# Wider tiles of the tensor engine in an audio tower: 64x128 projections, 64-column tiles for turned mixtures, output product and logits, 32x64 mixing

## The chip, the cores and the metric

One core of one Trainium2 chip runs the whole kernel in one launch. The metric is the device time of that launch in microseconds (us). All data are float32 but for two small causal masks in bfloat16.

## What is computed

The input is x of shape 128 x 64 x 750 (batch, feature, time). The result h has shape 128 x 94 x 64.

```python
# pooling to tokens: windows of 8 time steps, softmax of the window's scores
scores = einsum('bwkf,of->bwko', xp, w) + b
h = sum(xp * softmax(scores, axis=2), axis=2)                # (128, 94, 64)

# attention, 8 heads of rank 32, no causal mask
n = layernorm(h)
q, k = einsum('btd,hrd->bhtr', n, Q), einsum('bud,hrd->bhur', n, K)
attn = softmax(einsum('bhtr,bhur->bhtu', q, k) / sqrt(64), -1)
h = h + einsum('bhtd,hde->bte', einsum('bhtu,bud->bhtd', attn, n), VO)

# second layer: 4 heads of width 16, 4 experts each with its own query, causal
sx = einsum('bsh,ndh->bnsd', layernorm(h), hl_w) + hl_b
att = softmax(einsum('bnesd,bntd->bnest', q(sx, wq), k(sx, wk)) * 4 + causal, -1)
out = where(sx == 0, 0, einsum('bnest,bntd->bnesd', att, v(sx, wv)))
gs = softmax(einsum('bnsf,nef->bnse', out, gate_w) + gate_b, -1)
hn = layernorm(einsum('bnsed,bnse->bnsd', out, gs) + sx[n, n])   # the residual is batch n of head n
hx = masked two-layer net on hn; fout = layernorm(hx + hn)
h = h + fout * softmax(fout @ fgate_w.T, -1) per head
```

## The kernel before, in words

The batch is worked off in quads: four batch items at a time, 32 quads. The 94 tokens of an item are padded to 96 and cut into three blocks of 32, so that a tile of 128 partitions holds one block of four items. The work on one quad is spread over thirteen steps of a software pipeline that is written out by hand: each engine has a function `quad(g)`, called for g = 0 to 43, and in it stands, in a fixed order, what the engine does in that step, each piece for another quad (`g - 3`, `g - 7` and so on). Engines run their lists in order and meet only through semaphores; a wait stands before the piece that needs it. Nothing is moved at run time.

In step g TensorE (PE) does, in this order, with the line of the products in brackets:

- turns of exponentials for the second layer (turn_p3, L766), logits of the head (head_logits, L797), turns of x (turn, L588), a turn of fx (turn_rest, L803);
- mix3 (L776), the second layer's mixture over tokens, on 32x32 tiles;
- turn_x (L650), two more turn_p3, **turn_c(0)** (L785), score3_b (L752 the mask, L759 the scores), **turn_c(1)**, **turn_c(2)**, pool_x (L606, 128x32 tiles), front_turn (L703), two more turn_p3, layer1 (L807);
- **project** twice (L657), **front_pair(0)** (L710), front_sv (L716, L719), score(0) (L665), **front_pair(2)**, score(1), the last three functions on 64x32 tiles;
- **mix** (L676), layer2 (L811), score(2) (L665), **give_outT** (L686), with even g tok_score (L598, 128x32 tiles), with odd g a turn of token weights (L612), give_out (L697), score3_a (L737, L743), turns of x and of fo (L588, L790).

A tile is named rows x columns: rows are the partitions of the contraction, columns those of the weights and of the output. What the pieces in bold do:

- project: keys of the attention. The weights `g_w` have 128 columns of 64 rows, in two halves of the partitions. Before, a call takes four column tiles of 32 for each half: 8 products of 384 moving columns. ACT copies each call's result (copy_k, L1068); score(0) waits for both copies.
- front_pair: keys of the second layer for two experts, from weights `aq` of 4 heads x 32 columns: 8 products of 384 columns per call. ACT copies them (front_kp, L1101). mix waits for the copy of front_pair(2), whose banks it writes, and so does exp_s(0), which stands behind it in ACT's list.
- mix: attention weights times tokens, for 3 blocks, 2 parities of the heads, 2 halves of the 64 features and 4 items: 48 products of 384 columns on 32x32 tiles, weights `xn`. ACT copies the result (copy_cT, L1079) after exp_s(0) (L1074); exp_s(1), copy_oT, with odd g the copy of token weights, exp_s(2) follow.
- give_outT: the product with VO, accumulated over 4 pairs of heads: 16 products of 192 columns on 128x32 tiles.
- turn_c: turns the second layer's mixture back to tokens and applies a constant matrix `gx` with the gate's weights. For each of 4 experts and 4 blocks of 32 tokens the weights are a slice of `ct3`, in which the expert is the innermost dimension, and 84 columns of `gx` move: 16 products per call on 128x32 tiles.
- head_logits: 8 products of 12 columns on 96x32 tiles.

Two lines of layout matter for the steps:

```python
ct3 = sb("ct3", [128, NJ, 128, NE])        # NE = 4
xn = sb("xn", [128, 4, NJ, 2, NFEAT])      # NFEAT = 64
```

A float32 product appears in the trace as two MATMUL records and two LDWEIGHTS records (weight loads; engine PEld).

VectorE (DVE) holds the reductions, the shifts before exponentials (soft: L1368 the maximum, L1370 the subtraction), the guards (L1375) and transposes of 32x32 blocks (L1349). mix3 waits for soft(2), which needs score3_a. DVE also waits for layer2 in mask_second (L1440), after which score(2) may write its bank. ScalarE (ACT) holds exponentials and copies out of PSUM. GpSimd (POOL) holds elementwise work on SBUF; `residual` writes ft (z_made) and `norm_affine(.., 0, ..)` writes fx. SyncE (SP) issues two x loads of 375 KB per quad (L332) and eight stores (L380, L382). Instructions themselves come by DMA as well, through queues of the kind "instruction".

Of the kernel before, what the change touches and what calls it, by code (L numbers as in the profile page):

```python
# [15 lines left out]
TP = 96  # L16
HEADS, RANK = 8, 32
NH, NE, HD = 4, 4, 16
QB = 32
# [10 lines left out]
def exists(m, total):  # L30

    return not isinstance(m, int) or 0 <= m < total
# [10 lines left out]
def audio_tower(nc, x, tok_w, tok_b, attn_q, attn_k, attn_vo, hl_w, hl_b, wq, wk, wv, gate_w, gate_b,  # L43
                ln_g, ln_b, fc1_w, fc1_b, fc2_w, fc2_b, fnorm_g, fnorm_b, fgate_w, out):
    with ExitStack() as ctx:
# [7 lines left out]
        psum = ctx.enter_context(nc.psum_tensor("psum", [128, 8, 512], F32))  # L53
# [9 lines left out]
        g_w = sb("g_w", [128, 2, 128])  # L63
        vo_w = sb("vo_w", [128, HEADS // 2, NFEAT])
# [51 lines left out]
        HP = HEADS // 2  # L116
        TAIL = 29
        NT = 3
        TB = 32
        NJ = 3  # L120
# [6 lines left out]
        xn = sb("xn", [128, 4, NJ, 2, NFEAT])  # L127
        xT = sb("xT", [128, 2, 4, TP])
# [5 lines left out]
        pT = sb("pT", [128, NT, 2, HP, NT, TB])  # L134
        cT = sb("cT", [128, HP, NT, 4, TB])
        oT = sb("oT", [128, NT, 2, TB])
        cen = sb("cen", [HD, HD])
        aq = sb("aq", [128, NE, NH, 32])
# [8 lines left out]
        fgw = sb("fgw", [96, 2, NJ * NH])  # L147
        foT = sb("foT", [96, 256])
# [17 lines left out]
        x3T = sb("x3T", [128, 4, TP])  # L166
# [123 lines left out]
        z_made = sem("z_made")  # L290
# [17 lines left out]
        fo_made_late = sem("fo_made_late")  # L308
# [94 lines left out]
        def _(pool):  # L403
# [28 lines left out]
            for n in range(NH):  # L432
                rows = slice(QB * n, QB * n + QB)
# [67 lines left out]
            def norm_affine(g, k, done, order, dst):  # L501

                y = yc[:, k, :].rearrange("p (a d) -> p a d", d=HD)
                pool.tensor_tensor(y, y, bcast(gam[:, k, :], 1, NJ * NH), ALU.mult).then_inc(done, 1)
                pool.wait_ge(done, 2 * g + 1)
                y = yc[:, k, :].rearrange("p (" + order + " c) -> p " + order + " c", c=32, h=2)
                pool.tensor_tensor(dst, y,
                                   bcast(bcast(bet[:, k, :], 1, y.shape[2]), 1, y.shape[1]), ALU.add).then_inc(done, 1)
# [15 lines left out]
            def quad(g):  # L524
                if exists(g - 11, TAIL):
                    finish(g - 11)
                if exists(g, NQUAD):
                    if g < 4:
                        pool.wait_ge(tok_ready, (g) // 2 + 1)
                    weigh(g)  # L530
                if exists(g - 9, TAIL):
                    pool.wait_ge(z_mul, g - 8)
                    norm_affine(g - 9, 1, fo_made, "h j", fo[:, (g - 9) % FR, :].rearrange("p (j h c) -> p h j c", j=NJ, h=2))
                if exists(g - 2, NQUAD):
                    pool.wait_ge(at_summed, 3 * g - 3)
                    norm_p(1, at_normed)
                if exists(g - 2, NQUAD):
                    norm_p(2, at_normed)
                if exists(g - 6, NQUAD):
                    pool.wait_ge(y_eps, g - 5)  # L540
                    norm_power(g - 6, 0, y_rstd)
                if exists(g, NQUAD):
                    pool.wait_ge(ln_stat, 2 * g + 2)
                    ln_power(g)
                if exists(g - 6, TAIL):
                    pool.wait_ge(y_rstd, 2 * g - 10)
                    scale(0, y_mul)
                if exists(g - 5, NQUAD):
                    pool.wait_ge(l_inv, g - 4)
                    gate_scale((g - 5) % 2)  # L550
                if exists(g - 1, NQUAD):
                    pool.wait_ge(at_summed, 3 * g - 2)
                    norm_p(0, at_normed)
                if exists(g - 7, TAIL):
                    pool.wait_ge(t_made, g - 6)
                    residual()
                if exists(g - 8, NQUAD):
                    if g - 8 >= 28:
                        pool.wait_ge(z_eps, g - 7)
                    norm_power(g - 8, 1, z_rstd)  # L560
                if exists(g - 5, NQUAD):
                    pool.wait_ge(g_inv, 2 * g - 8)
                    gate_weight(g - 5)
                if exists(g - 6, TAIL):
                    norm_affine(g - 6, 0, fx_made, "j h", fx[:, :, 0:96].rearrange("p h (j c) -> p j h c", c=32))
                if exists(g - 5, NQUAD):
                    pool.wait_ge(g_weight, 2 * g - 8)
                    gate_mul((g - 5) % 2)
                if exists(g, NQUAD):
                    pool.wait_ge(ln_rstd, 2 * g + 2)  # L570
                    ln_apply(g, (g) % 4)
                if exists(g - 2, NQUAD):
                    pool.wait_ge(ln3_var, 2 * g - 2)
                    power3(g - 2)
                if exists(g - 8, TAIL):
                    scale(1, z_mul)
# [5 lines left out]
        def _(pe):  # L582
# [68 lines left out]
                mm.then_inc(at_turned, 1)  # L651

            def project(n, i, bank, done):
                for c in range(4):
                    for half in range(2):
                        rows = slice(64 * half, 64 * half + 64)
                        mm = pe.matmul(psum[32 * c:32 * c + 32, bank + half, 0:4 * TP], g_w[rows, i, 32 * c:32 * c + 32],  # L657
                                       xT[rows, n % 2, :, :].rearrange("p b t -> p (b t)"), start=True, stop=True)
                mm.then_inc(done, 1)

            def score(n, j, bank, done):
# [6 lines left out]

            def mix(n, bank):
                for ub in range(NT):  # L670
                    for par in range(2):
                        for c in range(2):
                            for b in range(4):
                                rows = slice(TB * b, TB * b + TB)
                                q = 64 * par + 32 * c
                                mm = pe.matmul(psum[q:q + 32, bank + b, 0:HP * TP].rearrange("p (h j t) -> p h j t", h=HP, j=NT),  # L676
                                               xn[rows, n % 4, ub, 0, 32 * c:32 * c + 32],
                                               pT[rows, :, par, :, ub, :].rearrange("p j h t -> p h j t"), start=(ub == 0), stop=(ub == NT - 1))
                mm.then_inc(at_mixed, 1)

            def give_outT(bank):
                for hp in range(HP):
                    for half in range(2):
                        for c in range(2):
                            q = 64 * half + 32 * c
                            mm = pe.matmul(psum[q:q + 32, bank, 0:NT * 64].rearrange("p (j c) -> p j c", j=NT), vo_w[:, hp, 32 * c:32 * c + 32],  # L686
                                           cT[:, hp, :, 2 * half:2 * half + 2, :].rearrange("p j b t -> p j (b t)"),
                                           start=(hp == 0), stop=(hp == HP - 1))
                mm.then_inc(at_outT, 1)

            def give_out(bank):
# [12 lines left out]
                mm.then_inc(f_turned, 1)  # L704

            def front_pair(e, bank, done):
                for n in range(NH):
                    for half in range(2):
                        rows = slice(64 * half, 64 * half + 64)
                        mm = pe.matmul(psum[32 * n:32 * n + 32, bank + half, 0:NJ * 128], aq[rows, e + half, n, :],  # L710
                                       x3T[rows, :, :].rearrange("p b t -> p (b t)"), start=True, stop=True)
                mm.then_inc(done, 1)

            def front_sv(bank):
# [65 lines left out]

            def turn_c(j, bank, done):
                for e in range(NE):
                    for b in range(4):
                        rows = slice(QB * b, QB * b + QB)
                        mm = pe.matmul(psum[rows, bank, GC * e:GC * e + GC], ct3[:, j, rows, e], gx[:, e, :], start=True, stop=True)  # L785
                mm.then_inc(done, 1)

# [4 lines left out]

            def head_logits(bank):
                for h in range(2):
                    for c in range(4):
                        rows = slice(QB * c, QB * c + QB)
                        mm = pe.matmul(psum[rows, bank, 0:NJ * NH], foT[:, 128 * h + QB * c:128 * h + QB * c + QB], fgw[:, h, :],  # L797
                                       start=(h == 0), stop=(h == 1))
                mm.then_inc(fl_made, 1)

# [468 lines left out]
        def _(dve):  # L1269
# [54 lines left out]
            for n in range(NH):  # L1324
                rows = slice(32 * n, 32 * n + HD)
# [129 lines left out]
            def quad(g):  # L1455
# [40 lines left out]
                if exists(g - 6, NQUAD):  # L1496
                    soft(g - 6, 1, 0, s_shifted1)
                if exists(g - 10, NQUAD):
                    if 1 <= g - 10 < 30:
                        dve.wait_ge(fo_made, 2 * g - 20)  # L1500
                    centre(g - 10)
# [95 lines left out]
```

## Time and profile before

| | |
|---|---|
| median of 3 runs | 1020.71 us (1018.73 to 1024.64) |
| profiled execution | 1028.39 us |
| its span, first to last instruction | 1026.7 us |
| mean granted clock of TensorE | 0.963 |
| busy: PE / DVE / ACT / POOL | 85% / 73% / 72% / 68% |
| PE records | 23616 matmul, 23616 weight load |

The chain is the work that ended last, followed back from the end; its shares say through which engine the end was reached. Busy time of PE is modelled: matmuls overlap, and the time of a record includes a latency during which the next one already streams. Idle time is listed before the instruction that ended it, with what released it; "issue" means that the engine waited for nothing that the profile shows.

### The profile page before, as it was taken

The page shows a single profiled execution, that of the slowest core. Times are in us where ns is not written, and L with a number is a line of the kernel's source. Part 1 is how long each engine was busy: PE and PEld are TensorE (multiplying, and loading weights), DVE is VectorE, ACT ScalarE, POOL GpSimd, SP SyncE. Part 2 cuts the span into 40 slices and gives each one's busy share as a digit, 9 for nine tenths or more (in the row PEclk, how much of TensorE's full clock was granted, in tenths as well). Part 3 has the DMA queues.
Part 4 walks back from the last instruction along what each step waited for, and adds up shares of the span by engine and source line. Part 5 has one row for each costly group of instructions (what it writes and reads, how often), then busy time and mean ns, then how long its engine had stood idle before and what let it go on. Part 6 is the DMA issues. An engine that isn't in the chain of part 4 may idle for free.

```text
span 1026.7 us, 53493 instructions
## 1 busy us (share of the span) xinstructions
PE 875.7 (85%) x23616; PEld 602.5 (59%) x23616; DVE 754.3 (73%) x1786; ACT 741.7 (72%) x2631; POOL 693.8 (68%) x1087
## 2 busy tenths in 40 slices
PE   4488988998898989899999999998998998887853
PEld 3365655665665656566676666665676665555531
DVE  2346677777777788778888788877888888776765
ACT  1567777887777888777887788887887787774521
POOL 3343345666678677677788777776777877766684
PEclk9789999999999999999999999999999999999965
DMA  6211111001111110011111111001000000000000
GB/s 191 66 62 33 33 34 33 27 11 33 33 33 37 38 36 24 18 38 37 38 38 38 37 37 38 15 27 41 7 9 7 7 7 7 4 8 6 11 8 21
DMA packets 34504, 31.47 MB, mean 31 GB/s; under 512 B 26080, under 2 KB 26080, under 8 KB 34272
## 3 DMA queue, kind: packets, MB, share of 16 engines
q1 hardware_dynamic: 33926, 28.00, 9.4%
q8 instruction: 185, 3.03, 1.2%
q14 instruction: 47, 0.39, 0.1%
q10 hardware_dynamic: 250, 0.05, 0.0%
q0 software_dynamic: 96, 0.00, 0.0%
HBM read 24.95 MB, written 3.08 MB: 27 GB/s over the span
## 4 chain that ended last, share of the span: by engine, by line
PE 62%; ACT 17%; DVE 11%; issue 4%; SPq 4%; POOL 2%; DMA 0%; POOLq 0%
PE psum L676 8%; ACT pu L1074 8%; PE psum L776 7%; PE psum L785 6%; PE psum L766 6%; PE psum L657 4%; PE psum L759 4%; PE psum L710 4%; DVE pu L1370 4%; DVE mx L1368 4%; ACT cT L1079 3%; PE psum L665 3%; SPq L346 2%; PE psum L606 2%; ACT kp L1101 2%
## 5 line engine op out<-in xcount | busy, mean ns | idle before, releaser
L1074 ACT ACTIVATE pu<-psum,mx 128x94 f32<-128x94 f32 x768 | 250.7, 386 | 4.0 <-DVE mx L1343 4.0
L1074 ACT ACTIVATION_READ_ACCUMULATOR pu<-psum,mx 128x1 f32 x768 | 194.7, 254 | 0.0
L462 POOL TENSOR_TENSOR pu<-pu,pr 128x752 f32<-128x752 f32 x96 | 137.4, 1445 | 23.9 <-DVE pr L1346 23.8
L1368 DVE TENSOR_REDUCE mx<-psum 128x16 f32<-128x1536 f32 (+2 forms) x96 | 117.2, 1221 | 48.3 <-PE psum L759 30.7
L495 POOL TENSOR_TENSOR st<-st,neg_half 128x12 f32<-128x12 f32 x64 | 146.2, 2285 | 5.0
L448 POOL TENSOR_TENSOR ln_ve<-ln_mv,eps_c 128x3 f32<-128x3 f32 x32 | 6.2, 193 | 178.8 <-DVE ln_mv L1338 178.8
L1343 DVE TENSOR_REDUCE mx<-psum 128x8 f32<-128x752 f32 x96 | 89.0, 927 | 46.1 <-PE psum L665 46.1
L1370 DVE TENSOR_TENSOR pu<-psum,mx 128x1536 f32<-128x1536 f32 (+2 forms) x96 | 117.6, 1225 | 3.3
L665 PE MATMUL psum<-kp,xT 64*32 64x376 f32 x1536 | 103.1, 486 | 17.4 <-DVE ft L1440 11.6
L1112 ACT ACTIVATE pT<-psum 128x512 f32<-128x512 f32 x192 | 104.5, 595 | 14.4 <-PE psum L766 12.5
L766 PE MATMUL psum<-ident_w,pu 128*128 128x128 f32 x768 | 102.1, 277 | 1.0 <-ACT pu L1074 0.6
L676 PE MATMUL psum<-pT,xn 32*32 32x384 f32 x3072 | 88.5, 491 | 9.6 <-ACT kp L1101 8.6
L1349 DVE STREAM_TRANSPOSE pT<-pu 128x768 f32<-128x768 f32 x96 | 89.7, 958 | 4.5 <-POOL pu L462 4.5
L766 PEld LDWEIGHTS psum<-ident_w,pu 128*128 128x128 f32 x768 | 87.6, 142 | 3.9 <-ACT pu L1074 1.2
L1375 DVE SCALAR_TENSOR_TENSOR ct<-sxT,psum 128x512 f32<-128x512 f32 x96 | 60.3, 684 | 32.3 <-PE psum L776 32.3
L785 PE MATMUL psum<-gx,ct 128*32 128x84 f32 x3072 | 74.1, 242 | 8.2 <-issue 6.7
L776 PE MATMUL psum<-pT,vv 32*32 32x384 f32 (+2 forms) x3072 | 70.9, 403 | 10.9 <-DVE pu L1370 9.7
L676 PEld LDWEIGHTS psum<-pT,xn 32*32 32x32 f32 x3072 | 45.2, 103 | 52.4 <-ACT kp L1101 30.7
L785 PEld LDWEIGHTS psum<-gx,ct 128*32 128x32 f32 x3072 | 61.9, 139 | 21.8 <-issue 19.5
L1115 ACT ACTIVATE oc<-psum 128x336 f32<-128x336 f32 x96 | 43.3, 452 | 38.8 <-PE psum L785 32.1
L1064 ACT ACTIVATE xT<-psum 128x384 f32<-128x384 f32 x32 | 15.7, 491 | 72.5 <-PE psum L650 72.4
L710 PE MATMUL psum<-x3T,aq 64*32 64x384 f32 x1024 | 65.8, 483 | 1.2 <-ACT hx L1121 1.2
(185 smaller groups left out, 2123.8 us busy)
## 6 DMA issues: line engine op xcount, KB each, us to landing
xs<-in_x SPq DMA_DIRECT2D x64, 375.0 KB, 3.8
out_h<-ho SPq DMA_DIRECT2D x126, 16.0 KB, 1.8
out_h<-ho SPq DMA_DIRECT2D x126, 7.5 KB, 1.8
gx<-in_L_ffn_gate_w SPq DMA_DIRECT2D x16, 0.2 KB
fc<-in_L_ffn_fc_w SPq DMA_DIRECT2D x12, 1.0 KB
fc<-in_L_ffn_fc_b SPq DMA_DIRECT2D x12, 0.1 KB
vo_w<-in_L_attn_VO SPq DMA_DIRECT2D x2, 64.0 KB, 8.7
q_w<-in_L_attn_Q SPq DMA_DIRECT2D x1, 64.0 KB, 7.8
```

The costliest lines, as they stand in the source:

```text
L462: pool.tensor_tensor(p, p, bcast(pr[:, j, :, :].rearrange("p a b -> p (a b)"), 2, NTOK), ALU.mult).then_inc(done, 1)
L495: pool.tensor_tensor(st[:, k, 3, :], st[:, k, 2, :], neg_half[:, 0:NJ * NH], ALU.pow).then_inc(rstd, 1)
L665: mm = pe.matmul(psum[TB * b:TB * b + TB, bank + par, 0:HP * NTOK], xT[rows, n % 2, b, TB * j:TB * j + TB], kp[rows, n % 2, b, :, 0:NTOK], ...
L676: mm = pe.matmul(psum[q:q + 32, bank + b, 0:HP * TP].rearrange("p (h j t) -> p h j t", h=HP, j=NT), xn[rows, n % 4, ub, 0, 32 * c:32 * c + ...
L710: mm = pe.matmul(psum[32 * n:32 * n + 32, bank + half, 0:NJ * 128], aq[rows, e + half, n, :], x3T[rows, :, :].rearrange("p b t -> p (b t)" ...
L766: mm = pe.transpose(psum[:, bank, 128 * e:128 * e + 128], pu3[j][:, e, k, :, :].rearrange("p b u -> p (b u)"), ident)
L776: mm = pe.matmul(psum[QB * n:QB * n + QB, bank + b, 128 * k:3 * 128].rearrange("p (j t e) -> p j e t", e=NE, t=QB), vv[rows, n3 % 2, k, n, ...
L785: mm = pe.matmul(psum[rows, bank, GC * e:GC * e + GC], ct3[:, j, rows, e], gx[:, e, :], start=True, stop=True)
L1074: ins = act.activation(pu[:, j, par, hp, 0:NTOK], psum[:, bank + par, NTOK * hp:NTOK * hp + NTOK], ACT.Exp, bias=mx[:, j, par, hp:hp + 1], ...
L1112: act.activation(pT3[:, SLOT3[P3[f]], :, :].rearrange("p e c -> p (e c)"), psum[:, bank, :], ACT.Exp).then_inc(done, 1)
L1368: dve.tensor_reduce(mx3[:, j, :, :], S3(j, bank), AX.X, ALU.max).then_inc(shifted, 1)
L1370: dve.tensor_tensor(pu3[j][:, :, :, :, :].rearrange("p e k b u -> p b e k u"), S3(j, bank).rearrange("p b e (k u) -> p b e k u", u=QB), bc ...
```

## The change

project and front_pair give each half of the partitions one product of 128 columns instead of four of 32 (8 products become 2 per call). mix takes the 64 features in one product instead of two (48 become 24) and has the loop over items outside that over parities. give_outT, turn_c and head_logits go over two column tiles of 64 instead of four of 32 (16 become 8, 16 become 8 in each of three calls, 8 become 4). The order of the pieces in every engine's list is the same. Two waits are added: POOL waits for its own residual before norm_affine, and DVE for its own late normalization before centre, in the last two quads.

```diff
@@ pool, quad(g)
                 if exists(g - 6, TAIL):
+                    if g - 6 >= 1:
+                        pool.wait_ge(z_made, g - 6)
                     norm_affine(g - 6, 0, fx_made, "j h", fx[:, :, 0:96].rearrange("p h (j c) -> p j h c", c=32))
@@ project
-                for c in range(4):
-                    for half in range(2):
-                        rows = slice(64 * half, 64 * half + 64)
-                        mm = pe.matmul(psum[32 * c:32 * c + 32, bank + half, 0:4 * TP], g_w[rows, i, 32 * c:32 * c + 32],
-                                       xT[rows, n % 2, :, :].rearrange("p b t -> p (b t)"), start=True, stop=True)
+                for half in range(2):
+                    rows = slice(64 * half, 64 * half + 64)
+                    mm = pe.matmul(psum[:, bank + half, 0:4 * TP], g_w[rows, i, :], xT[rows, n % 2, :, :].rearrange("p b t -> p (b t)"),
+                                   start=True, stop=True)
@@ mix
                 for ub in range(NT):
-                    for par in range(2):
-                        for c in range(2):
-                            for b in range(4):
-                                rows = slice(TB * b, TB * b + TB)
-                                q = 64 * par + 32 * c
-                                mm = pe.matmul(psum[q:q + 32, bank + b, 0:HP * TP].rearrange("p (h j t) -> p h j t", h=HP, j=NT),
-                                               xn[rows, n % 4, ub, 0, 32 * c:32 * c + 32],
-                                               pT[rows, :, par, :, ub, :].rearrange("p j h t -> p h j t"), start=(ub == 0), stop=(ub == NT - 1))
+                    for b in range(4):
+                        rows = slice(TB * b, TB * b + TB)
+                        for par in range(2):
+                            mm = pe.matmul(psum[64 * par:64 * par + 64, bank + b, 0:HP * TP].rearrange("p (h j t) -> p h j t", h=HP, j=NT),
+                                           xn[rows, n % 4, ub, 0, :], pT[rows, :, par, :, ub, :].rearrange("p j h t -> p h j t"),
+                                           start=(ub == 0), stop=(ub == NT - 1))
@@ give_outT
                     for half in range(2):
-                        for c in range(2):
-                            q = 64 * half + 32 * c
-                            mm = pe.matmul(psum[q:q + 32, bank, 0:NT * 64].rearrange("p (j c) -> p j c", j=NT), vo_w[:, hp, 32 * c:32 * c + 32],
...
+                        mm = pe.matmul(psum[64 * half:64 * half + 64, bank, 0:NT * 64].rearrange("p (j c) -> p j c", j=NT), vo_w[:, hp, :],
...
@@ front_pair
-                for n in range(NH):
-                    for half in range(2):
-                        rows = slice(64 * half, 64 * half + 64)
-                        mm = pe.matmul(psum[32 * n:32 * n + 32, bank + half, 0:NJ * 128], aq[rows, e + half, n, :],
-                                       x3T[rows, :, :].rearrange("p b t -> p (b t)"), start=True, stop=True)
+                for half in range(2):
+                    rows = slice(64 * half, 64 * half + 64)
+                    mm = pe.matmul(psum[:, bank + half, 0:NJ * 128], aq[rows, e + half, :, :].rearrange("p n d -> p (n d)"),
+                                   x3T[rows, :, :].rearrange("p b t -> p (b t)"), start=True, stop=True)
@@ turn_c
                 for e in range(NE):
-                    for b in range(4):
-                        rows = slice(QB * b, QB * b + QB)
+                    for h in range(2):
+                        rows = slice(64 * h, 64 * h + 64)
                         mm = pe.matmul(psum[rows, bank, GC * e:GC * e + GC], ct3[:, j, rows, e], gx[:, e, :], start=True, stop=True)
@@ head_logits
-                    for c in range(4):
-                        rows = slice(QB * c, QB * c + QB)
-                        mm = pe.matmul(psum[rows, bank, 0:NJ * NH], foT[:, 128 * h + QB * c:128 * h + QB * c + QB], fgw[:, h, :],
+                    for c in range(2):
+                        rows = slice(64 * c, 64 * c + 64)
+                        mm = pe.matmul(psum[rows, bank, 0:NJ * NH], foT[:, 128 * h + 64 * c:128 * h + 64 * c + 64], fgw[:, h, :],
                                        start=(h == 0), stop=(h == 1))
@@ vector, quad(g)
                 if exists(g - 10, NQUAD):
+                    if g - 10 >= 30:
+                        dve.wait_ge(fo_made_late, 2 * g - 78)
```

## Rows read from the trace of the kernel before

**Rows 1.** The page: busy time and the chain's shares.

```profile
PE 875.7 (85%) x23616; PEld 602.5 (59%) x23616; DVE 754.3 (73%) x1786; ACT 741.7 (72%) x2631; POOL 693.8 (68%) x1087
PE 62%; ACT 17%; DVE 11%; issue 4%; SPq 4%; POOL 2%; DMA 0%; POOLq 0%
```

**Rows 2.** Windows: us; busy (x) of PE, PEld, DVE, ACT, POOL; clock, DMA share, GB/s.

```profile
497.83:512.63 14.80, 14.52 (x460) 10.84 (x460) 12.63 (x30) 10.76 (x25) 11.12 (x18) 1.00 0.21 62
512.63:525.45 12.82, 11.88 (x296) 7.90 (x297) 10.27 (x27) 12.35 (x58) 11.18 (x18) 1.00 0.01 4
...
540.25:552.85 12.60, 11.00 (x249) 6.69 (x250) 10.24 (x27) 12.20 (x59) 10.78 (x17) 1.00 0.01 4
```

**Rows 3.** The chain of waits, 495 to 556 us: start, length, what.

```profile
511.77 0.82 ACT kp L1101
...
512.63 2.77 PE psum L676 x94
...
521.75 1.77 DVE mx L1368
...
543.05 1.51 ACT cT L1079 x2
```

**Rows 4.** Timeline of PE, 500 to 512 us: start, length, records.

```profile
501.23 0.82 PE L785 MATMUL psum<-gx,ct 128*32 128x84 f32 x32
...
503.45 1.40 PE L785 MATMUL psum<-gx,ct 128*32 128x84 f32 x64
504.66 0.85 PE L606 MATMUL psum<-xt,wp 128*32 128x64 f32 x48
...
506.70 0.60 PE L807 MATMUL psum<-fxT,fc 128*128 128x256 f32 x2
507.23 1.52 PE L657 MATMUL psum<-xT,g_w 64*32 64x384 f32 x32
508.55 0.85 PE L710 MATMUL psum<-x3T,aq 64*32 64x384 f32 x16
509.19 0.48 PE L716 MATMUL psum<-x3T,wsx 64*32 64x384 f32 x1
...
510.55 0.52 PE L665 MATMUL psum<-kp,xT 64*32 64x376 f32 x2
...
511.19 0.53 PE L710 MATMUL psum<-x3T,aq 64*32 64x384 f32 x2
```

**Rows 5.** Groups by line and shape, weight loads: busy us, mean ns.

```profile
L785 PEld LDWEIGHTS psum<-gx,ct 128*32 128x32 f32 x3072 | 61.9, 139 | 21.8 <-issue 19.5 <-DVE ct L1375 1.6 <-ACT oc L1115 0.7
L686 PEld LDWEIGHTS psum<-cT,vo_w 128*32 128x32 f32 x1024 | 30.0, 109 | 30.5 <-ACT cT L1079 24.2
L811 PEld LDWEIGHTS psum<-fc,hxm 128*128 128x128 f32 x128 | 17.5, 198 | 28.6 <-ACT pu L1074 16.3 <-DVE hxm L1436 11.1 <-issue 1.2
```

**Rows 6.** Timeline of weight loads, layer2.

```profile
515.33 0.52 PEld L811 LDWEIGHTS psum<-fc,hxm 128*128 128x128 f32 x4 [0.62 <-ACT pu L1074]
```

**Rows 7.** Timeline of ACT around mix.

```profile
514.90 0.25 ACT L1074 ACTIVATION_READ_ACCUMULATOR pu<-psum,mx 128x1 f32 x1
515.43 0.81 ACT L1079 ACTIVATE cT<-psum 128x768 f32<-128x768 f32 x1 [0.28 <-PE psum L676]
```

**Rows 8.** Instruction supply: queue, waits over the run, timelines of PE and SP.

```profile
q8 instruction: 185, 3.03, 1.2%
...
PE psum L606 <- issue: 13.0, 13, 1.4
...
PE psum L785 <- issue: 6.7, 6, 1.6
...
PE psum L759 <- issue: 3.5, 4, 1.7
...
693.72 0.83 SPq L332 DMA_DIRECT2D xs<-in_x  x2
...
787.75 0.77 PE L606 MATMUL psum<-xt,wp 128*32 128x64 f32 x40 [1.14 <-issue]
```

More of the change, by code:

```diff
@@ L683, in give_outT @@
                     for half in range(2):
-                        for c in range(2):
-                            q = 64 * half + 32 * c
-                            mm = pe.matmul(psum[q:q + 32, bank, 0:NT * 64].rearrange("p (j c) -> p j c", j=NT), vo_w[:, hp, 32 * c:32 * c + 32],
-                                           cT[:, hp, :, 2 * half:2 * half + 2, :].rearrange("p j b t -> p j (b t)"),
-                                           start=(hp == 0), stop=(hp == HP - 1))
+                        mm = pe.matmul(psum[64 * half:64 * half + 64, bank, 0:NT * 64].rearrange("p (j c) -> p j c", j=NT), vo_w[:, hp, :],
+                                       cT[:, hp, :, 2 * half:2 * half + 2, :].rearrange("p j b t -> p j (b t)"),
+                                       start=(hp == 0), stop=(hp == HP - 1))
                 mm.then_inc(at_outT, 1)
```

## The prediction, made before any run of the changed kernel

> **What bounds the kernel now.** The page comes first: PE is busy for 85% of the span, and 62% of the chain that ended last is PE's, 17% ACT's, 11% DVE's, 4% "issue" [rows 1]. Matmuls overlap, so a busy share proves no limit; the windows show where PE is one. A quad in steady state has two stretches: 14.80 us from the first product of mix3 to that of mix, and 12.82 (even g) or 12.60 us (odd g) from mix to the next mix3 [rows 2]. In the first PE is busy for 14.52 of 14.80 us, and in the chain of waits it is PE alone until a single ACT copy of 0.82 us: what PE gains or loses there is the quad's. In the second the chain goes through others: with even g mix, layer2, DVE, PE, then DVE's passes over the scores (the first 1.77 us); with odd g ACT's copies of mix (1.51 us) and the exponentials behind them [rows 3]. The granted clock is 1.00 in both, the level of 2.4 GHz.
>
> **How PE spends its time.** A float32 product is two records and two weight loads. turn_c takes 0.82 us for 32 records and 1.40 for 64 [rows 4], so 32 more cost 0.58 us: with four column tiles abreast, 8 waves of 0.0725 us. The 84 moving columns, twice, at 2.4 GHz are 0.070. So waves, not instructions, cost time: four tiles of 32 or two of 64 need the same number of waves. In the products that change the waves stay at 8 per turn_c call, 2 per projection, 6 in mix, 8 in outT, 4 in the logits. The change removes 84 products per quad (12 in project, 12 in front_pair, 24 in mix, 8 in outT, 24 in turn_c, 4 in the logits), that is 336 PE instructions, but not a streamed column per tile. What is left is (a) the weight loads, wider now, (b) array shapes that alternate more often, (c) stagger and instruction supply.
>
> **(a) turn_c's loads.** A load of 32 columns lasts 109 ns in outT and 139 in turn_c, on the same shape of tile [rows 5]. The weights differ in one thing: `ct3[:, j, rows, e]` takes every fourth float. layer2's load of 128 adjacent columns lasts 198 ns [rows 5], so a column costs (198-109)/96 = 0.93 ns and the fixed part is 79; turn_c's 32 cost 60, or 1.9 each, so 64 cost about 120: a load like layer2's. How fast such loads follow each other is shown by layer2: four in 0.52 us, the last starting 0.32 after the first, steps of 0.107, though its 96 columns stream in 0.080 [rows 6]. Loads of 107 ns aren't hidden under 72 ns of streaming. turn_c then goes at 0.11 us per wave: 24 waves x 0.0375 = +0.90 us per quad. Bounds: 0, if a 64-column load stays under the stream, to 24 x (0.12-0.0725) = +1.14. I take +0.90, since layer2 is the nearest row; 32 quads, +28.8 us. The other wider loads hide: 64 adjacent columns (about 60 ns) under mix's waves of 0.32 us and outT's of 0.16. The logits stream 12 columns, so their four waves become load-bound, +0.1 us; they run while PE waits for DVE or ACT ahead of mix3. Without that cover it would be 3 us in all.
>
> **(b) Changes of shape.** Where the shape stays (L657 to L710), the next group starts 0.20 us before the modelled end of the last; where it changes (L807 to L657), 0.07 before [rows 4]: 0.13 us each time. turn_c to pool_x (L785 to L606) kept a shape of four column tiles, 0.19 before the end; now it doesn't: +0.13 us, less 0.03 where score3_b already waits for DVE. +0.10 x 29 = +3 us. outT to tok_score likewise on even g.
> The front costs more. Today project, front_pair, front_sv, score(0) and score(1) are all on 64x32 tiles, and front_pair(2) slips between the scores. A wave of 384 columns, twice, is 0.32 us; a record lasts 0.48, so 0.16 is latency to the modelled end. Count from project's first record S = 507.23 [rows 4]. New: first load of 128 columns 0.11, six waves of 0.32, drain 0.09: front_sv begins at S+2.14 (today 1.96). front_sv with score(0) keeps its 1.72 us (509.19 to 511.07 less the latency [rows 4]) and adds 0.02 for a first load, so PE is empty at S+3.88; a drain of 0.09, a load of 0.11, two waves of 0.32 and 0.16 to the modelled end: front_pair(2) is complete at S+4.89, today at 511.72, S+4.49. ACT's copy, for which mix waits, starts right at that end today (511.77) [rows 3]. So +0.40 us per quad, 30 quads, +12 us; score(1) follows on PE beside the copy. Bounds: +0.08 (the first load alone) to +0.55 (a full 0.13 for each of three changes, plus the load).
>
> **(c) mix and what follows.** Its 96 records take 2.77 us [rows 3]; six waves of 0.32, a load and the latency are 2.2, so PE gets 0.56 us back. The chain gets less: copy_cT waits only 0.28 us for mix [rows 7], then exp_s(0) itself is the bound. Odd g: -0.25. Even g: layer2 waits for exp_s(0) too, which ends at 515.15 [rows 7] against layer2's start at 515.33 [rows 6]: about -0.12, and the change before tok_score gives 0.15 back: +0.03. Mean -0.11, 30 quads, -3 us. If mix's gain all counted it would be -17.
>
> **(d) Instruction supply.** The instruction queue moves 3.03 MB in 185 packets, 256 instructions each. In some quads PE stops for "issue" inside turn_c, score3_b or pool_x; over the run these are 13.0 + 6.7 + 3.5 us in 23 stops [rows 8], and with the 0.2 us that the modelled ends cover, 28 us. From turn_c(0) to pool_x 424 instructions go in 4.2 us (501.23 to pool_x's last start at about 505.4 [rows 4]), a block in 2.5; with stops of about 1.3 a block seems to need 3.8. New: 328 in 5.2 us, 256 in 4.1. I estimate that 20 of the 28 us go; what stays are blocks due while a quad's x load and stores run, as they do around mix3 (DMA share 0.21 against 0.01 later in the quad [rows 2]). Bounds 0 and -28.
> The Trainium skill (Runtime: NRT & Kernel Launch, Instruction fetch mechanics) has such crossings as mostly hidden. By it this term is nothing and the sum comes out 20 us higher.
>
> POOL's new wait is for its own residual, which already stands ahead in its queue; DVE's concerns the last two quads. Behind POOL's stand gate_mul and ln_apply; the cover is POOL's idle time, busy for 68% [rows 1] and for 11.1 of 14.8 us in the tight stretch [rows 2]. I cost both at 0; a few tenths in the tail if not.
>
> **Sum**: 28.8 + 3 + 12 - 3 - 20 = +21 us. The profiled execution took 1028.4 us (span 1026.7), so 1049 there; the median of the runs is 7.7 lower, which gives 1042.
>
> **Rivals.**
> R1, faster: a 64-column load in turn_c stays under the stream. Place: L785; it decides at 72 ns. Then 21 - 29 = -8: 1013. For it: 32 columns hide today and nothing in the trace is a strided load of 64. Against: 139 against 109 ns. 
> R2: the stops for "issue" stay, because a block is late through the x load and not through PE's rate: +41, 1062. Against: the last x load is issued at 693.72, and pool_x still stops for 1.14 us at 787.75 [rows 8].
> R3: turn_c's loads cost about half of what I say (8 to 20 us in all), or mix's full gain reaches the chain: 1020 to 1030.
> R4: the change doesn't do what it says. Fewer products is certain from the diff; less streaming, which "larger" suggests, is not there.
>
> **How the numbers follow.** Forecast 0.57 (its own range 1031 to 1054), R1 0.20, R2 0.10, R3 0.13. A measurement tells about 0.5%, 5 us, from no change. Slower: 0.57 + 0.10 + a third of R3 = 0.71; same: the rest of R3 and the edge of R1, 0.11; faster 0.18. The range 1012 to 1060 leaves out half of R1 and most of R2.
>
> **What would show it.** turn_c's load groups some 190 to 200 ns long and its 64 records now 32 in about 1.9 us; front_sv starting 2.14 us after project; the copy after front_pair(2) 0.4 later; mix near 2.2 us, but copy_cT still waiting, now for nothing of PE; idle for "issue" at L785 and L606 largely gone; the first stretch near 16.1 us, the second near 12.7. Wrong, if turn_c keeps 0.82 us, or if the first stretch stays under 15.3.

## The result and the profile after

The changed kernel takes 1038.86 us (median of 4 runs, 1036.44 to 1041.36) against 1021.62 us for the kernel before in the same comparison: ratio 1.0163, 95% interval 1.0125 to 1.0200. It is slower by 17 us; 21 were forecast. The profiled execution took 1041.36 us, its span 1039.6. Two executions in the rounds below were slow and enter no median: one of the kernel before (1073.32 us, granted clock 0.83) and one of e3_ct3_flat (1951.31 us).

The page: busy time, the chain's shares, the instruction queue.

```profile
PE 913.4 (88%) x18240; PEld 612.9 (59%) x18240; DVE 754.5 (73%) x1786; ACT 742.0 (71%) x2631; POOL 696.5 (67%) x1087
PE 59%; ACT 24%; DVE 9%; SPq 4%; POOL 2%; issue 1%; DMA 0%; POOLq 0%
...
q8 instruction: 143, 2.34, 0.9%
```

5376 matmul records fewer than in [rows 1], 168 in each of 32 quads, are two for each of the 84 products that went. PE is nevertheless busy for 38 us more, and "issue" has shrunk from 4% of the chain to 1%. Those are the two sides of the result. Stops while matmuls wait for issue, 23.2 us in [rows 8], are no longer in the list of waits at all; weight loads still show short ones:

```profile
PEld psum L781 <- issue: 11.0, 60, 0.2
```

The windows, cut as in [rows 2] at mix3's and at mix's first product:

```profile
525.61:542.04 16.43, 16.31 (x365) 11.39 (x365) 12.91 (x32) 10.72 (x25) 10.53 (x16) 1.00 0.18 56
542.04:554.24 12.20, 10.52 (x177) 6.46 (x178) 9.71 (x25) 12.08 (x59) 11.05 (x18) 1.00 0.01 3
554.24:570.67 16.43, 16.31 (x365) 11.38 (x366) 12.93 (x32) 10.84 (x25) 10.97 (x17) 1.00 0.18 56
570.67:583.50 12.83, 11.43 (x224) 7.59 (x225) 10.31 (x25) 12.35 (x58) 11.38 (x18) 1.00 0.01 3
```

The first stretch has grown from 14.80 to 16.43 us, and PE, busy for 16.31 of them, is its bound more than before. The second is 12.20 us with odd g, where it was 12.60, and 12.83 with even g, where it was 12.82. The chain (start, length, what) has the same two quads, 28.63 and 29.26 us long:

```profile
525.61 2.12 PE psum L772 x73
...
541.17 0.81 ACT kp L1097
541.99 2.57 ACT pu L1070 x16
544.55 1.40 ACT cT L1075 x2
...
554.24 2.11 PE psum L772 x74
...
570.61 2.58 ACT pu L1070 x16
...
579.81 1.77 DVE mx L1364
...
583.50 0.51 PE psum L772 x2
```

Before, they were 27.40 (odd g) and 27.62 us (even g) where no stop fell into them [rows 2]. mix itself has left the chain: ACT goes from exp_s(0) straight to copy_cT, where it waited before [rows 7].

PE's timeline in the first stretch (start, length, records):

```profile
529.01 1.19 PE L781 MATMUL psum<-gx,ct 128*64 128x84 f32 x16
...
531.57 2.15 PE L781 MATMUL psum<-gx,ct 128*64 128x84 f32 x32
533.65 0.88 PE L608 MATMUL psum<-xt,wp 128*32 128x64 f32 x48
...
536.24 1.56 PE L658 MATMUL psum<-xT,g_w 64*128 64x384 f32 x8
537.63 0.81 PE L706 MATMUL psum<-x3T,aq 64*128 64x384 f32 x4
538.38 0.51 PE L712 MATMUL psum<-x3T,wsx 64*32 64x384 f32 x1
...
540.21 0.92 PE L706 MATMUL psum<-x3T,aq 64*128 64x384 f32 x4
...
542.04 2.19 PE L675 MATMUL psum<-pT,xn 32*64 32x384 f32 x48
```

Beside [rows 4]: turn_c's calls take 1.19 and 2.15 us for 0.82 and 1.40, with half the records. Sixteen records more cost 0.96 us, 8 waves of 0.120 (a wave is one record on each of the two column tiles). From project's first record, front_sv starts at +2.14 us and front_pair(2) is complete at +4.89 (541.13). mix takes 2.19 us for 2.77.

Weight loads by line and shape (busy us, mean ns), beside [rows 5]:

```profile
L781 PEld LDWEIGHTS psum<-gx,ct 128*64 128x64 f32 x1536 | 97.3, 215 | 13.3 <-issue 11.0 <-DVE ct L1371 1.6 <-ACT oc L1111 0.7
...
L683 PEld LDWEIGHTS psum<-cT,vo_w 128*64 128x64 f32 x512 | 33.9, 136 | 26.8 <-ACT cT L1075 23.2
```

On the same tile of 64 columns, adjacent floats load in 136 ns and every fourth in 215.

### The profile page after: what moved, and what is told of

Read it like the earlier page. It is cut to its first block, busy times and chain, and to the rows that moved or that the text cites. A ratio compares the mean times of both kernels' runs of the same rounds, so it can differ in the third digit from the quotient of the medians.

```text
span 1039.6 us, 42741 instructions
## 1 busy us (share of the span) xinstructions
PE 913.4 (88%) x18240; PEld 612.9 (59%) x18240; DVE 754.5 (73%) x1786; ACT 742.0 (71%) x2631; POOL 696.5 (67%) x1087
## 4 chain that ended last, share of the span: by engine, by line
PE 59%; ACT 24%; DVE 9%; SPq 4%; POOL 2%; issue 1%; DMA 0%; POOLq 0%
ACT pu L1070 15%; PE psum L781 10%; PE psum L772 7%; PE psum L762 6%; PE psum L706 5%; PE psum L658 4%; PE psum L755 4%; DVE pu L1366 4%; DVE mx L1364 4%; PE psum L666 3%; ACT cT L1075 3%; SPq L346 2%; ACT kp L1097 2%; PE psum L608 2%; PE psum L683 2%; PE psum L712 2%
## 5 line engine op out<-in xcount | busy, mean ns | idle before, releaser
L1070 ACT ACTIVATE pu<-psum,mx 128x94 f32<-128x94 f32 x768 | 254.3, 425 | 4.0 <-DVE mx L1339 4.0
L1070 ACT ACTIVATION_READ_ACCUMULATOR pu<-psum,mx 128x1 f32 x768 | 215.3, 293 | 0.0
L1108 ACT ACTIVATE pT<-psum 128x512 f32<-128x512 f32 x192 | 104.5, 595 | 14.6 <-PE psum L762 12.9
L666 PE MATMUL psum<-kp,xT 64*32 64x376 f32 x1536 | 94.3, 489 | 19.3 <-DVE ft L1436 11.6
L781 PE MATMUL psum<-gx,ct 128*64 128x84 f32 x1536 | 107.2, 289 | 1.3 <-DVE ct L1371 0.8
L781 PEld LDWEIGHTS psum<-gx,ct 128*64 128x64 f32 x1536 | 97.3, 215 | 13.3 <-issue 11.0
L675 PE MATMUL psum<-pT,xn 32*64 32x384 f32 x1536 | 70.2, 490 | 4.4 <-ACT kp L1097 0.9
L1097 ACT ACTIVATE kp<-psum 128x768 f32<-128x768 f32 x64 | 52.0, 812 | 23.8 <-PE psum L706 23.6
L772 PEld LDWEIGHTS psum<-pT,vv 32*32 32x32 f32 x3072 | 45.6, 106 | 38.1 <-ACT xt L1057 16.2
```

The lines of the kernel that those rows point to most:

```text
L666: mm = pe.matmul(psum[TB * b:TB * b + TB, bank + par, 0:HP * NTOK], xT[rows, n % 2, b, TB * j:TB * j + TB], kp[rows, n % 2, b, :, 0:NTOK], ...
L772: mm = pe.matmul(psum[QB * n:QB * n + QB, bank + b, 128 * k:3 * 128].rearrange("p (j t e) -> p j e t", e=NE, t=QB), vv[rows, n3 % 2, k, n, ...
L1070: ins = act.activation(pu[:, j, par, hp, 0:NTOK], psum[:, bank + par, NTOK * hp:NTOK * hp + NTOK], ACT.Exp, bias=mx[:, j, par, hp:hp + 1], ...
L1108: act.activation(pT3[:, SLOT3[P3[f]], :, :].rearrange("p e c -> p (e c)"), psum[:, bank, :], ACT.Exp).then_inc(done, 1)
```

## The experiments

Microseconds saved or lost against the kernel before refer to its median in the same rounds: 1023.47 us for e1 to e4, 1023.04 for e5 to e8, 1023.33 for e9.

**Which part costs what: one part undone, or done alone.** First turn_c, undone in the changed kernel:

```diff
 def turn_c(j, bank, done):
-    for h in range(2):
-        rows = slice(64 * h, 64 * h + 64)
+    for b in range(4):
+        rows = slice(QB * b, QB * b + QB)
```

> The changed kernel with turn_c alone back on four column tiles of 32. Theory (strided 64-column loads set turn_c's pace, 0.12 us per wave against 0.0725, and its slow pace also gives the instruction supply its time): a quad without a stop gets 24 x 0.0475 + 0.1 = 1.24 us shorter, about 27.4 (odd g) and 28.0 (even g), some -37 us in all, but stops for issue of 1 to 2 us come back in about half of the quads, +15 to +28 us: 1017 to 1030 us against 1038.9. Rival (loads of 64 columns are not the cause, the cost sits in the front's shapes): the quad keeps 28.6 and 29.3 us and the time stays within 5 us of the changed kernel. Rival (the supply follows the total number of instructions, which stays 16% below the first kernel's): quads 1.24 us shorter and hardly any stops, near 1002.

Measured: 1029.8 us (ratio to the kernel before 1.0071, 1.0043 to 1.0098). The chain has quads without a stop of 27.40 us (403.37 to 430.77) and 28.04 us (722.23 to 750.27), 1.23 and 1.22 less than in the changed kernel:

```profile
403.37 2.12 PE psum L772 x73
430.77 2.12 PE psum L772 x73
...
722.23 2.12 PE psum L772 x72
750.27 2.12 PE psum L772 x73
```

and the waits for issue are back, 16.6 us in those of 0.4 us and more:

```profile
PE psum L608 <- issue: 8.4, 9, 1.5
...
PE psum L781 <- issue: 6.9, 10, 1.1
PE psum L762 <- issue: 0.9, 1, 0.9
...
PE psum L748 <- issue: 0.4, 1, 0.4
```

Both rivals fall: the cost is turn_c's, and the stops return although the kernel still has 16% fewer PE instructions than the first. Of the 37 us forecast from the quads only 9 reach the end.

The reverse, turn_c alone changed in the kernel before (the same lines):

> The kernel before with turn_c alone on two column tiles of 64. Theory: quads at 27.4 and 27.6 us become 28.65 and 28.85 without a stop, +37 us; turn_c issues 96 fewer of the 424 instructions of its region in 1.2 us more, so nearly all of the 28 us of stops go: about 1030 us, 9 above the kernel before. Rival (stops come from the x load alone and not from PE's rate): the 28 us stay, 1058 us. Rival (a 64-column load stays under the stream): no longer quads and fewer stops, under 1015.

Measured: 1034.51 us (1.0117, 1.0070 to 1.0165). Quads of 28.64 us (838.44 to 867.08) and 28.85 us (723.46 to 752.31), +1.24 and +1.23, and a single stop is left:

```profile
723.46 2.12 PE psum L776 x72
752.31 2.12 PE psum L776 x73
...
838.44 2.12 PE psum L776 x73
867.08 2.12 PE psum L776 x73
```

```profile
PE psum L785 <- issue: 1.4, 1, 1.4
```

The x load is where it was; what changed is PE's pace in the region. From turn_c(0) to pool_x's last start it asks for 328 instructions in 5.3 us, where it asked for 424 in 4.1. So the stops need a PE that asks for instructions sooner than they come; what the load's traffic adds is tried below.

The front, project and front_pair back on 64x32 tiles in the changed kernel:

```diff
-for half in range(2):
-    mm = pe.matmul(psum[:, bank + half, ...], g_w[rows, i, :], ...)
+for c in range(4):
+    for half in range(2):
+        mm = pe.matmul(psum[32 * c:32 * c + 32, bank + half, ...], g_w[rows, i, 32 * c:32 * c + 32], ...)
```

> The changed kernel with project and front_pair alone back on 64x32 tiles. Theory (three changes of shape and a first load of 128 columns put front_pair(2)'s end 0.40 us later in each quad): quads of 28.2 and 28.85 us, no stops, 12 us less in all: 1027 us. Rival (wide tiles are free there, all of the loss is turn_c's): within 3 us of 1038.9. Rival (the 96 instructions more per quad bring stops back): quads 0.4 us shorter but stops of over 1 us in some of them, 1033 or more.

Measured: 1025.87 us, 13.0 less than the changed kernel, or 15 by the two ratios (ratio to before 1.0014, 0.9988 to 1.0041). Quads of 28.24 us (403.18 to 431.42) and 28.87 us (431.42 to 460.29): -0.39 both, as the theory had it, and one wait for issue of 0.4 us. How the 0.39 us divides between the changes of shape and the wider first load was not tried.

```profile
403.18 2.12 PE psum L774 x73
431.42 2.12 PE psum L774 x73
460.29 2.12 PE psum L774 x73
```

mix, done alone in the kernel before:

```diff
-for par in range(2):
-    for c in range(2):
-        for b in range(4):
-            ... xn[rows, n % 4, ub, 0, 32 * c:32 * c + 32] ...
+for b in range(4):
+    for par in range(2):
+        ... xn[rows, n % 4, ub, 0, :] ...
```

> The kernel before with mix alone on 32x64 tiles. Theory (mix gives PE 0.56 us back, but the chain only what copy_cT and layer2 had waited for it beyond exp_s(0)): quads without a stop go from 27.40 and 27.62 us to about 27.1 (odd g) and 27.5 (even g), -6 us in all; the stops for issue stay near 28 us, because mix lies outside their region: 1015 to 1018 us. Rival (the whole 0.56 us reaches the chain): 26.9 and 27.1, 1005 us. Rival (fewer instructions anywhere mean fewer stops): stops under 20 us, 1008 or less.

Measured: 1017.01 us (0.9935, 0.9910 to 0.9961), 6 us faster. Quads without a stop: 27.00 us (odd g) and 27.49 us (even g).

```profile
403.01 2.12 PE psum L774 x72
430.01 2.12 PE psum L774 x73
...
713.76 2.12 PE psum L774 x73
741.25 2.12 PE psum L774 x73
```

The waits for issue sum to 20.3 us: they stay. Even g gained 0.13 as forecast, odd g 0.40 where 0.25 was. The forecast took the 0.28 us of idle before copy_cT, which counts from the end of exp_s(0)'s last record. Before, copy_cT started 0.53 us after the start of that record [rows 7]; in the changed kernel, as here, it starts 0.10 after it, inside the record's time:

```profile
544.30 0.25 ACT L1070 ACTIVATION_READ_ACCUMULATOR pu<-psum,mx 128x1 f32 x1
544.40 1.56 ACT L1075 ACTIVATE cT<-psum 128x768 f32<-128x768 f32 x2
```

That is 0.43 us earlier.

mix and give_outT together, against mix alone:

```diff
-for c in range(2):
-    q = 64 * half + 32 * c
-    ... vo_w[:, hp, 32 * c:32 * c + 32] ...
+... vo_w[:, hp, :] ...
```

> The kernel before with mix on 32x64 and give_outT on 128x64 tiles. Theory: even quads 0.15 us longer than those of e5_mix_only, because give_outT and tok_score no longer share a shape, odd quads the same. Rival (the change of shape is hidden there): both as e5_mix_only.

Measured: a single run, of 1017.71 us; quads of 26.99 us (odd g, 464.51 to 491.50) and 27.64 (even g, 717.96 to 745.60), 0.15 more than with mix alone where tok_score follows, nothing where it doesn't. The change of shape costs what it was priced at, as far as one profile tells.

**Why turn_c's loads are long.** The changed kernel with ct3 stored expert by expert:

```diff
-ct3 = sb("ct3", [128, NJ, 128, NE])
+ct3 = sb("ct3", [128, NJ, NE, 128])
...
-out=ct3[:, j, :, :].rearrange("p (b t) e -> p b t e", b=4)
+out=ct3[:, j, :, :].rearrange("p e (b t) -> p b t e", b=4)
...
-ct3[:, j, rows, e]
+ct3[:, j, e, rows]
```

> The changed kernel with ct3 laid out expert by expert, so that turn_c's weights are 64 adjacent floats; VectorE's guard writes it with a larger stride. Theory (stride, not width, makes the load long): turn_c's loads fall from 215 ns to about 135, its waves from 0.12 to 0.0725 us, the quad by 1.2 us to about 27.4 and 28.05; -36 us. With 328 instructions in 4.1 us some stops for issue may come back, 0 to 10 us: 1003 to 1013 us. Rival (width makes it long, whatever the stride): turn_c stays at 0.12 us per wave and the time at 1038. Rival (VectorE pays for the stride in the guard, 0.68 us each today): guards of over 0.9 us, score3_b waits for them and half of the gain is lost, 1020 to 1025.

Measured: 1038.54 us, the median of three runs (1038.08 to 1043.89; ratio 1.0165, 1.0106 to 1.0225): the mechanism confirmed, the gain nil. The timeline of PE, the group of loads, and VectorE's guard:

```profile
527.71 0.80 PE L781 MATMUL psum<-gx,ct 128*64 128x84 f32 x16
529.50 0.29 PE L748 MATMUL psum<-causB,causA 32*128 32x256 bf16 x4 [0.99 <-DVE ct L1371]
530.93 1.38 PE L781 MATMUL psum<-gx,ct 128*64 128x84 f32 x32
```

```profile
L781 PEld LDWEIGHTS psum<-gx,ct 128*64 128x64 f32 x1536 | 60.1, 139 | 14.5 <-DVE ct L1371 7.1 <-issue 6.1 <-ACT oc L1111 1.2
...
L1371 DVE SCALAR_TENSOR_TENSOR ct<-sxT,psum 128x512 f32<-128x512 f32 x96 | 92.2, 1065 | 36.0 <-PE psum L772 36.0
```

The loads fall from 215 to 139 ns and turn_c to 0.80 and 1.38 us, 0.0725 per wave: stride, not width. But the guard now writes with the large stride and takes 1065 ns for 683; the three of a quad run one behind the other, 2.89 us from 526.47, and score3_b's mask now waits 0.99 us for the last. From turn_c(0) to pool_x PE takes 4.5 us where it took 4.6, and the quads are 28.54 and 29.16 us, 0.1 shorter than in the changed kernel. That is nearly all of turn_c's gain gone; I had put the price of this rival at half.

**What the stops for issue hang on.** In the kernel before, SyncE holds its x load and stores of a step back until mix is done; nothing is left out:

```diff
 sp.wait_ge(x_turned, 3 * g + 3)
+if g >= 2:
+    sp.wait_ge(at_mixed, g - 1)
 load(g + 6)
```

> The kernel before with SyncE's x load and stores of each step held back until mix of that step is done; nothing else. If instruction blocks come late because a load and the stores fill the 16 DMA engines just ahead of the dense region: quads of 30 to 31 us become 27.4 to 29, the stops fall from 28 to about 15 us, 1008 to 1012 us. If the block's own latency against PE's rate makes all of the stops: no change, within 4 us of the kernel before. If the load is now late for tok_score or the stores for the next result: longer quads with PE waiting for a DMA.

Measured: 1010.25 us (0.9882, 0.9846 to 0.9918), 12.8 us faster. The x loads are issued about 18 us after mix3's first record, where they were issued within half a microsecond of it. Over the run the waits for issue are 9.9 us, not 23.2, and none is over 1.1 us:

```profile
PE psum L608 <- issue: 7.9, 12, 1.0
...
PE psum L787 <- issue: 2.0, 2, 1.1
```

The quads without a stop are still 27.40 and 27.62 us. That these waits are for instruction blocks is shown by where they fall. From 150 to 920 us the kernel before has 25 stops of over 0.3 us in the region, this run 15, and all 15 stand at the same places, counted in PE's records: 5535, 8332, 9857, 12654 and so on. Where a quad had two stops, 254 or 255 records apart, the first of the two is gone. And in both runs PE goes on 1.2 to 1.7 us after the last packet of the instruction queue has ended, each time. Whether the load or the stores matter more was not taken apart.

The two gains together, mix on 32x64 tiles and the late load:

> The kernel before with mix on 32x64 tiles, and with SyncE's x load and stores of each step held back until mix of that step is done, so that they run in the second stretch of the quad. Nothing is left out. If the load's traffic makes instruction blocks late: stops of over 1.5 us vanish and the total falls from 28 to under 15 us, 1000 to 1006 us. If PE's own rate is all: as e5_mix_only, 1015 to 1018.

Measured: 1004.40 us (0.9823, 0.9787 to 0.9860). 6 and 13 us add up. The two largest waits for issue come to 13.1 us. This version is faster than both kernels.

The control, the late load in the changed kernel, which has no stops to lose:

> The changed kernel with SyncE's x load and stores of each step held back until mix of that step is done. If holding the load back helps only through the stops for issue, of which the changed kernel has none left: quads stay at 28.63 and 29.27 us and the time within 3 us of 1038.9. If it helps the quad in another way too (ports, the load's own timing): 5 us or more less, below 1034. If the traffic disturbs the second stretch: longer quads, above 1042.

Measured: 1036.42 us (1.0131, 1.0091 to 1.0171), within 3 us of the changed kernel; quads stay at 28.63 us (405.12 to 433.75) and 29.25 (433.75 to 463.00). So holding the load back helps through the stops, and any other effect is under about 3 us.

```profile
405.12 2.11 PE psum L774 x73
433.75 2.12 PE psum L774 x73
463.00 2.12 PE psum L774 x74
```

## Why the prediction was right

By quads without a stop, the parts measured one at a time add up to the whole:

| part | forecast per quad | odd g | even g | shown by |
|---|---|---|---|---|
| turn_c, with pool_x's change of shape | +1.00 | +1.24 | +1.23 | e2_turnc_only |
| project and front_pair | +0.40 | +0.39 | +0.39 | e4_front_back |
| mix | -0.25 / -0.12 | -0.40 | -0.13 | e5_mix_only |
| give_outT before tok_score | 0 / +0.15 | 0 | +0.15 | e7_mix_outt |
| sum | +1.29 mean | +1.23 | +1.64 | |
| changed kernel less the kernel before | | +1.23 | +1.64 | chain |

- (a) turn_c. The mechanism held: a 64-column load with a stride of four floats isn't hidden. It was mis-sized: a wave takes 0.120 us, the upper bound, not 0.11, which makes +1.14 us a quad where +0.90 was forecast. The extrapolation by columns (60 ns for 32, 120 for 64) was nearer than layer2's row, from which I took the value. With pool_x, which starts 0.07 us before turn_c's modelled end instead of 0.19, it is 1.24 us, an estimated 37 us over 30 quads where 32 were forecast. R1 falls with 215 ns against 136 on the same tile. The Trainium skill (SBUF — State Buffer, Door 1: The DMA port swizzle) has 16-byte lines in that memory, of which each must be hit at least twice in a row for full rate; a stride of four floats hits each once. The trace agrees as to the stride, 215 ns with it and 139 without; that lines are the reason is not shown here. By the Trainium skill (TensorE: Matmul & The Clock Gate, LDWEIGHTS) P columns take P/1.2 ns, 27 ns for 32 columns more. The traces agree for adjacent columns, 109 to 136 ns, and not for strided ones, 139 to 215.
- (b) The front. S+2.14 and S+4.89 came out to the hundredth, and undoing it gave 13 us back where 12 were. The hundredths are luck: the terms as written add up to S+2.12 and S+4.88.
- (c) mix. PE got its 0.58 us, the chain 0.40 and 0.13; layer2 now waits 0.37 us for exp_s(0) and not for mix. Mean with give_outT -0.19, -6 us, where -3 were forecast.
- (d) Instruction supply, the term that was furthest off: all of the 28 us (23.2 of them in the list of waits) went, not 20. I had kept 8 us for blocks that fall due during the x load. e2_turnc_only shows that the slower turn_c alone leaves 1.4 us; e8_before_lateload shows that the traffic is real, worth 13 us while PE is fast, and that 9.9 us of waits stay without it. R2 is thus half true, as a part of the cause, and wrong as a forecast: with PE slow, the load where it was makes hardly a stop. The Trainium skill's "mostly hidden" (Runtime: NRT & Kernel Launch, Instruction fetch mechanics) doesn't hold for the kernel before, with 23.2 us of such waits, and holds for the changed one.
- The sum. From the first mix3 to the twenty-ninth, 28 quads, the two profiled executions differ by 7.4 us (119.25 to 920.55 us, 121.13 to 929.83). Only 11 of these quads have the even form, the others the odd one, so the table gives +39.0 us (17 x 1.23 + 11 x 1.64), and the stops that went were worth about 31.6 us in the one profiled before. Each of the two executions also has one stretch of 3.4 us at the clock's lower level in these quads (granted 0.50 from 414.9 to 418.3 us before the change), which was not taken out. The filling adds 1.9 and the tail 3.6, 12.9 in all; that the tiles cause these two is not shown, since with the same tiles e9_after_late has its first mix3 at 116.44 us. Against the medians, 17.2 apart, the stops come to 22 us, or 27 if filling and tail are put down to the tiles. The forecast had the tiles at 40.8 us (28.8 + 3 + 12 - 3) and the stops at -20. In it turn_c was some 5 us too cheap, mix's gain some 3 us too small and the gain from the stops 2 to 12 too small, on opposite sides, and that the total came within 4 us is in part luck.
- POOL's and DVE's new waits: the list of waits has none of POOL or DVE for work of their own there, and the quads are accounted for without them.

## What to carry to other kernels

Merging narrow tiles into wide ones removed instructions here, not streaming time: with all column tiles busy the number of waves was the same. What decides is whether the wider weight load still hides under one wave (of 64 columns, the strided one took 215 ns and the adjacent one 139), and how many changes of array shape are added between groups that used to share one. Before a product is sped up, see what its consumer waits for behind it: mix gave PE 0.58 us and the quad 0.27. Where a dense run of small PE instructions coincides with a large DMA, move the DMA: one more wait in SyncE's list gained 13 us, where the best of the tiles, mix, gained 6.

## What was not expected of the hardware

- Instructions arrive in blocks of about 255 (47232 records of PE in 185 packets before, 36480 in 143 after). They are late when PE takes 424 in 4.1 us and not when it takes 328 in 5.3 (529.01 to pool_x's last start at 534.30). It is no sharp bound: with 328 in 5.2 us, in e3_ct3_flat, there are three stops of 1.5 us together. The same stops shrink from 23.2 to 9.9 us when nothing changes but the time at which 750 KB of loads and the stores run.
- VectorE's guard takes 683 ns when it writes 512 adjacent floats and 1065 ns when it writes them 128 floats apart, with the same reads.
